# Delta-rule stage: ScalarE takes the key squares before the outputs, three engines share the copies of the inverse, and the first inverse product stands in slot 9

## The chip, the cores and the metric

One core of one Trainium2 chip. The metric is the device time of one execution in microseconds, as the median of several runs.

## What is computed

The whole program is four blocks of attention and feed-forward on x of shape 2 x 1024 x 256, each added to its input. The change lies in the attention of the last block, a gated delta rule with 32 heads of 64 and a convolution of four taps over time:

```python
mixed = lax.conv_general_dilated(mixed, conv_w, (1,), [(K_CONV - 1, 0)], ...)
...
g = -jnp.exp(A_log) * jax.nn.softplus(a + dt_bias)
beta = jax.nn.sigmoid(b)
q = _l2norm(q) * DK ** (-0.5)
k = _l2norm(k)
...
def step(Sstate, xs):
    q_t, k_t, v_t, g_t, b_t = xs
    Sstate = Sstate * jnp.exp(g_t)[..., None, None]
    kv = jnp.einsum('bhk,bhkv->bhv', k_t, Sstate)
    delta = (v_t - kv) * b_t[..., None]
    Sstate = Sstate + k_t[..., :, None] * delta[..., None, :]
    o_t = jnp.einsum('bhk,bhkv->bhv', q_t, Sstate)
    return (Sstate, o_t)
...
o = o * lax.rsqrt(var + EPS) * norm_weight * jax.nn.sigmoid(z)
return o.reshape(Bsz, Sl, VDIM) @ w_out.T
```

## The kernel before

heads3 works through 32 units: a pair of heads (16) times a sequence (2). The 1024 tokens of a unit are 16 chunks of 64. Within a chunk the recurrence is solved by the inverse of a 64 x 64 unit lower triangular matrix I + N (nT is N transposed); from chunk to chunk a state st of 64 x 64 for each head is carried.

The program is a software pipeline written out by hand. Each engine has its own instruction list, made of start, step and end, and meets the others only through counting semaphores; each engine works strictly in the order of its list. A call of step(t, u, f, p) serves four units at once: p is being projected and convolved, f gets its decays, its N and its inverse, u runs through its 16 states, t is normalised, gated and projected out. The loop body is two steps; on TensorE it is cut in the middle of a step, between slots 7 and 8 (CUT), so that its loop branch falls there in every second unit.

TensorE's step has two halves. The key side (key_side) transposes the keys of f, sums its decays (decay), and interleaves the products of keys of f (key_products) with the products of the inverse of u with values and keys (values_and_keys, key_sums). Then states runs 16 slots c = 0 to 15. In each slot the state of chunk c comes in (across), the products of the next chunk that need no state follow (within), and then beside(c) puts other work in: projections, the inverse of f, the output of t. A state needs the one before it, so across(c) waits for VectorE's update of state c, called state c or q = c - 1 here.

The inverse of f goes so: ScalarE copies the diagonal 32 x 32 blocks of nT together in y (compacted, four copies by quarters of the partitions), VectorE transposes and folds them down to 16 x 16 blocks (diagonals, gather), GpSimd solves these by 15 double steps on [128, up to 64] elements (solve) and writes them scaled as xm and xmT (sided), VectorE transposes them back (scatter) to xx. TensorE doubles them with products of 32 x 32: inverse_y, then VectorE masks; inverse_z and inverse_zt, and VectorE subtracts (refined); inverse_below, a copy into y, inverse_above, a copy into xT. These copies were ScalarE's alone (inverse_pieces): two into y, four of xx into xT, a table load, two of the product above into xT. values_and_keys of the next step needs xT whole.

Other orders that the change touches: on ScalarE, outputs (copies and squares of the finished outputs, banks 4 and 5) ended a step, and key_squares began the next; its query_squares wait for GpSimd's squares (the sum of output squares and query terms). On GpSimd a step is squares, scaled (decay times beta), gated, solve, sided, gates. PSUM banks 2 and 3 (B3), 0 and 1 (A3), 4 and 5 (C3), 6 and 7 (D3) are shared out by hand; POUT names the banks of the four output projections.

## Time and profile before

| | |
|---|---|
| median of 3 runs | 5064.07 us (5057.12 to 5071.15) |
| the profiled execution | 5072.44 us, its span 5070.4 us |
| TensorE matmul (PE) busy | 4314.5 us, 85% |
| VectorE (DVE) busy | 2256.2 us, 44% |
| ScalarE (ACT) busy | 1796.4 us, 35% |
| GpSimd (POOL) busy | 1150.8 us, 23% |
| mean granted clock of TensorE | 0.870 of full |

"[1.38 <-ACT h_y L2843]" behind an instruction says that its engine stood idle for 1.38 us before it, and which instruction released it; "issue" names no one. A little product of the inverse has many matmuls, so a row with x64 is a whole group. The units of the stage take 59.7 us each; line L3060 (VectorE's copy of the first state) occurs once in each.

### The profile page before, as it was taken

To read this page: it belongs to the slowest core of one execution; us is meant where nothing else is said; L and a number is where in the kernel's file an instruction comes from. 1 tells how busy PE (TensorE), PEld (TensorE's weight loads), DVE (VectorE), ACT (ScalarE), POOL (GpSimd) and SP (SyncE) were. 2 spreads that over 40 slices of the span, in tenths; PEclk is the share of its full clock that TensorE was granted. 3 is DMA by queue.
4 is the path that set the end of the run, shared out by engine and by line. 5 is a ranking of instruction groups with operands and counts; after the bars stand their busy time and mean duration, and the time that the engine had idled before them with its cause. 6 is when DMAs were issued, how large, how long until landed. Compare 5 with 4: busy or idle time off the path is not lost. (4 is left out here: it accounts for less than half of the span.)

```text
span 5070.4 us, 110954 instructions
## 1 busy us (share of the span) xinstructions
PE 4314.5 (85%) x45765; PEld 2627.0 (52%) x45824; DVE 2256.2 (44%) x3826; ACT 1796.4 (35%) x2794; POOL 1150.8 (23%) x1633
## 2 busy tenths in 40 slices
PE   7789869999967858779998789899988888889879
PEld 3233744544544634446466555555555555555547
DVE  5933244334443252431322255565556555555431
ACT  2057121221220113231110245555555555555431
POOL 2000110000015241310000144444444444444300
PEclk8689679999978967889998679998999998898878
DMA  1000000000021510000100000000000000000000
GB/s 43 1 1 1 26 33 1 9 9 0 3 86 52 173 52 0 0 21 0 51 0 5 9 7 9 8 8 8 8 8 8 8 8 8 8 8 8 6 13 17
DMA packets 37871, 91.96 MB, mean 18 GB/s; under 512 B 6914, under 2 KB 27173, under 8 KB 33920
## 3 DMA queue, kind: packets, MB, share of 16 engines
q1 hardware_dynamic: 27072, 69.45, 4.0%
q0 software_dynamic: 6144, 11.62, 0.8%
q8 instruction: 386, 6.32, 0.5%
q10 hardware_dynamic: 4224, 4.19, 0.3%
q14 instruction: 45, 0.37, 0.0%
HBM read 69.96 MB, written 20.45 MB: 18 GB/s over the span
## 5 line engine op out<-in xcount | busy, mean ns | idle before, releaser
L2426 PE MATMUL ps<-h_normT,h_w 128*128 128x512 f32 (+1 forms) x1008 | 456.1, 560 | 62.2 <-DVE h_xx L3001 55.9
L2943 DVE SCALAR_TENSOR_TENSOR h_cv<-h_raw,h_cw,h_cv 128x1023 f32<-128x1023 f32 (+2 forms) x288 | 371.3, 1299 | 22.3 <-ACT h_cv L2776 19.6
L3062 DVE SCALAR_TENSOR_TENSOR h_st<-h_st,d_gcs,ps 128x64 f32<-128x64 f32 x448 | 125.0, 279 | 493.8 <-PE ps L2701 493.3
L2775 ACT ACTIVATE h_raw<-ps 128x512 f32<-128x512 f32 x192 | 114.8, 598 | 529.9 <-PE ps L2426 529.0
L2335 POOL TENSOR_TENSOR h_gm<-h_gm,h_tmp 128x15 f32<-128x15 f32 (+7 forms) x480 | 260.5, 543 | 37.6
L2343 POOL TENSOR_TENSOR h_sq<-h_sq,h_qsq 128x512 f32<-128x512 f32 x64 | 79.9, 1270 | 806.8 <-ACT h_sq L2922 806.8
L877 PE MATMUL ps<-a_probT,a_v 128*128 128x512 f32 x512 | 232.5, 613 | 25.1 <-DVE a_probT L939 25.1
L2426 PEld LDWEIGHTS ps<-h_normT,h_w 128*128 128x128 f32 x1008 | 172.7, 201 | 156.1 <-issue 137.0
L854 PE MATMUL ps<-a_qkT 128*128 128x512 f32 x512 | 230.0, 593 | 3.1 <-DVE a_v L930 3.1
L2701 PEld LDWEIGHTS ps<-h_st,h_mT 64*64 64x64 f32 x1792 | 93.5, 137 | 245.3 <-issue 239.7
L1922 PE MATMUL ps<-h_normT,e_wgu 128*128 128x512 f32 (+1 forms) x448 | 204.3, 600 | 5.2 <-DMA e_wd<-in_e_wd 4.0
L2334 POOL TENSOR_TENSOR h_tmp<-h_gm 128x15 f32<-128x15 f32 (+7 forms) x480 | 179.0, 373 | 129.2 <-DVE h_gm L2988 94.1
L944 DVE TENSOR_REDUCE a_nmax<-ps 128x1 f32<-128x1024 f32 x64 | 78.4, 1224 | 240.3 <-PE ps L854 240.3
L2701 PE MATMUL ps<-h_st,h_mT 64*64 64x64 f32 x1792 | 152.6, 247 | 36.7 <-issue 27.4
L877 PEld LDWEIGHTS ps<-a_probT,a_v 128*128 128x128 f32 x512 | 99.1, 196 | 149.7 <-issue 120.1
L1086 POOL MEMSET r_zero<- 128x2048 f32 x1 | 1.8, 1804 | 766.3 <-POOLq L54 766.3
L2496 PE MATMUL ps<-h_wo,h_o 128*128 128x256 f32 x512 | 170.7, 452 | 5.5 <-DVE h_o L3007 3.8
L407 ACT ACTIVATE a_prob<-ps 128x1024 f32<-128x1024 f32 (+1 forms) x192 | 153.9, 810 | 59.9 <-PE ps L335 21.2
L448 DVE TENSOR_REDUCE a_mx<-ps 128x2 f32<-128x1024 f32 (+2 forms) x192 | 169.0, 950 | 1.8 <-PE ps L296 1.0
L909 ACT ACTIVATE a_prob<-ps,a_nbias 128x1024 f32<-128x1024 f32 x64 | 71.3, 1114 | 275.4 <-DVE a_nbias L946 275.4
L2705 PE MATMUL ps<-h_pT,h_st 64*64 64x64 f32 x1920 | 166.1, 252 | 0.5 <-DVE h_st L3062 0.5
L148 PE MATMUL ps<-ident,h_norm 128*128 128x128 f32 x256 | 48.7, 378 | 134.2 <-DVE h_norm L127 134.2
(515 smaller groups left out, 9587.2 us busy)
## 6 DMA issues: line engine op xcount, KB each, us to landing
m_wgu<-in_m_wgu SPq DMA_DIRECT2D x8, 1408.0 KB
h_w<-in_d_w SPq DMA_DIRECT2D x48, 128.0 KB, 2.1
m_wd<-in_m_wd SPq DMA_DIRECT2D x8, 704.0 KB
m_rows_in<-r_zero SPq DMA_DIRECT2D x4, 1024.0 KB, 12.2
e_xe<-m_rows_in SPq DMA_DIRECT2D x8, 512.0 KB
m_rows_out<-e_y ACTq DMA_DIRECT2D x8, 512.0 KB, 11.4
e_wgu<-in_e_wgu SPq DMA_DIRECT2D x1, 3520.0 KB
a_t_raw<-in_t_w SPq DMA_DIRECT2D x4, 768.0 KB, 4.4
```

The costliest lines, as they stand in the source:

```text
L407: act.activation(prob[:, u % 3, :, c0:BANK], ps[:, 2 * (u % 3):2 * (u % 3) + 2, c0:BANK], ACT.Exp, scale=1.0 / float(np.sqrt(D0))).then_in ...
L448: dve.tensor_reduce(mx[:, b * NQ + qt, part, m:m + 5:4], ps[:, 2 * (n % 3):2 * (n % 3) + 2, 0:w], AX.X, ALU.max).then_inc(mx_ready, 1)
L854: last = pe.matmul(ps[:, 2 * (n % 2) + half, :], qkT[:, 0, k, n * P:(n + 1) * P], qkT[:, 1, k, b * S + half * BANK:b * S + (half + 1) * BANK],
L877: last = pe.matmul(ps[:, 6 + m, :], v[:, b * NQ + kt, m * P:(m + 1) * P], probT[:, blk % 2, kt, :], start=(kt == 0), stop=(kt == NQ - 1))
L1922: last = pe.matmul(ps[0:m, 3 * (n % 2) + s, :], wgu[:, k, s, c * P:c * P + m], hT[:, k, tok], start=(k == 0), stop=(k == KC - 1))
L2334: c.link(pool.tensor_tensor(part, column, row, ALU.mult))
L2335: c.link(pool.tensor_tensor(target, target, part, ALU.subtract))
L2426: last = pe.matmul(ps[:, PROJ[m], lo:hi], w[:, kind, k, :], hT[:, k, b * S + tb * BANK + lo:b * S + tb * BANK + hi], start=(k == 0), stop= ...
L2496: last = pe.matmul(ps[:, POUT[k], j * H:(j + 1) * H], o[:, tile * P:(tile + 1) * P], wo[:], start=True, stop=True)
L2701: last = pe.matmul(ps[rows(h), D3 + c % 2, 0:HALF], mT[rows(h), c, :], st[rows(h), c, :], start=False, stop=True, tile_position=(64 * h, 6 ...
L2705: last = pe.matmul(res(h, c), st[rows(h), c, :], pT[rows(h), c, :], start=False, stop=True, tile_position=(64 * h, 64 * (1 - h)))
L2943: dve.scalar_tensor_tensor(out=d, in0=raw[:, kind, 0:S - back], scalar=tap(pr, kind, TAPS3 - 1 - back), in1=d, op0=ALU.mult, op1=ALU.add). ...
```

## The change

- TensorE: inverse_y stands in slot 9 instead of 10 and the value transposes in slot 8 instead of 9. The output projections 1, 2, 3 of t go from slots 8, 11 and 13 to 10, 12 and 13, with other banks (POUT). inverse_z goes to slot 11, inverse_zt to 12, inverse_below to 13, ahead of output projection 3; inverse_above stays in 14, alone.
- ScalarE: key_squares and decays come first in a step, then outputs of t, then the first wc and u copies and one query square; the second query square stands behind decays_upto. compacted makes three of four quarters; inverse_pieces loads its table first and makes one of two copies into y, two of four from xx, one of two from the product above.
- GpSimd: solve begins with the fourth quarter of compacted (waiting for gated and for nT), spread makes the other two copies of xx into xT behind gates.
- VectorE: the last quarter of the copy into y (below, in slot 14) and of the product above (above, at the end of the step); nT's second half is made ahead of the paired product of the second half; the transposes (scatter) move from slot 10 to 8, values to 9, masked to 10, the second gate to 11, the additions and convolutions by a slot or two.

The diff, cut to its core (the waits of the first and last steps, of start and of end are left out):

```diff
         MEAN = (A3, A3 + 1)
-        POUT = (B3 + 1, B3 + 1, A3, A3)
+        POUT = (B3 + 1, A3, A3, B3)
         UW = (D3, C3)
         KK = (A3, B3)
...
+        one = lambda r: ct[quarter(r), SUM.start + r // 2 * HALF:SUM.start + r // 2 * HALF + 1].unsqueeze(1).broadcast_to([32, NC3, DB2])
         SUBS = 2 * DB3 - 1
         blocks = lambda v: v.rearrange("p c (h j) -> p j h c", h=2)
...
                     pool.wait_ge(dec_d, 2 * n + 2)
                     pool.tensor_tensor(dec[:, grp(g), :], dec[:, grp(g), :], per_chunk(bep[:, grp(g)]), ALU.mult).then_inc(db_d, 1)
-            def solve(f):
+            def solve(f, t=None):
                 n = f[0]
                 c = Chain(pool, sub, SUBS * n)
                 eye = ct[:, EYE3]
+                pool.wait_ge(rz, 2 * t[0] + 2) if t else pool.wait_ge(db_d, 2 * n + 2)
+                pool.wait_ge(nt_d, 2 * n + 2)
+                pool.tensor_tensor(y[quarter(3), :, :], nT[quarter(3), :, side(3)], one(3), ALU.mult).then_inc(nc3_d, 1)
+                pool.wait_ge(nc3_d, n + 1)
                 pool.wait_ge(eg_p, 2 * n + 2)
                 c.link(pool.tensor_tensor(xb, eye, eye, ALU.mult))
...
                     c.link(pool.tensor_tensor(target, target, part, ALU.subtract))
                 assert c.n == SUBS
+            def spread(f, p):
+
+                pool.wait_ge(gm_d, 2 * p[0] + 2) if p else pool.wait_ge(xm_d, 2 * f[0] + 2)
+                pool.wait_ge(x_d, 2 * f[0] + 2)
+                for r in (1, 3):
+                    pool.tensor_tensor(xT[quarter(r), :, side(r)], xx[quarter(r), 1, :, :], one(r), ALU.mult).then_inc(xt_d, 1)
+                pool.wait_ge(xt_d, 2 * f[0] + 1 + r // 2)
+
             def squares(t):
                 n, pr, b = t
...
                     last.then_inc(wk, 1)
+                if t:
+                    hold(xa, 4 * n)
                 if f:
                     hold(ev, 6 * f[0] + 6)
                     hold(x_d, 2 * n + 2)
                     turn_keys(f)
-                if t:
-                    hold(xa, 4 * n)
-                if f:
                     hold(y4_d, 2 * n + 2)
                     decay(f)
-                hold(xtx, 6 * n + 6)
+                hold(xtx, 4 * n + 4)
+                hold(xt_d, 2 * n + 2)
                 hold(v_ev, n + 1)
                 if t:
...
-                    if c == 8 and t:
-                        pe.wait_ge(xa, 4 * n + 1)
-                        project_out(t, 1)
-                    if c == 9 and f:
+                    if c == 8 and f:
                         hold(ev, 6 * p[0] + 4) if p else hold(lnd, 2 * t[0] + 2)
                         turn_values(f)
-                    if c == 10 and f:
+                    if c == 9 and f:
                         if p:
-                            pe.wait_ge(xa, 4 * n + 2) if t else pe.wait_ge(ev, 6 * p[0] + 2)
+                            pe.wait_ge(xa, 4 * n + 1) if t else pe.wait_ge(ev, 6 * p[0] + 2)
                         hold(zv, 2 * n + 2)
                         inverse_y(f, (lambda k: project(p, 4, k)) if p else None)
-                    if c == 11 and t:
+                    if c == 10 and t:
                         pe.wait_ge(v_ev, f[0] + 1) if f else pe.wait_ge(lnd, 2 * t[0] + 2)
-                        project_out(t, 2)
-                    if c == 12 and f:
+                        project_out(t, 1)
+                    if c == 11 and f:
                         hold(v_ev, f[0] + 1)
                         inverse_z(f, (lambda k: project(p, 5, k)) if p else None)
+                    if c == 12:
+                        if t:
+                            pe.wait_ge(xa, 4 * n + 2)
+                        if f:
+                            hold(ev, 6 * p[0] + 5) if p else hold(xa, 4 * n + 1)
+                            inverse_zt(f, (lambda k: out_part(t, 2, k // 2) if k % 2 else None) if t else None)
+                        elif t:
+                            project_out(t, 2)
                     if c == 13:
+                        if f:
+                            inverse_below(f)
                         if t:
-                            pe.wait_ge(xa, 4 * n + 3)
-                        if f:
-                            hold(ev, 6 * p[0] + 5) if p else hold(xa, 4 * n + 2)
-                            inverse_zt(f, (lambda k: out_part(t, 3, k // 2) if k % 2 else None) if t else None)
-                        elif t:
+                            pe.wait_ge(ev, 6 * p[0] + 6) if p else pe.wait_ge(zv, 2 * n + 2)
                             project_out(t, 3)
                     if c == 14 and f:
-                        inverse_below(f)
                         inverse_above(f)
...
             def inverse_pieces(f):
                 n = f[0]
+                act.preload_act_table(ACT.Exp)
                 act.wait_ge(nx, 2 * n + 2)
-                for r in (1, 3):
-                    act.activation(y[quarter(r), :, :], small(BELOWB)[quarter(r)], ACT.Copy).then_inc(y4_d, 1)
+                act.activation(y[quarter(1), :, :], small(BELOWB)[quarter(1)], ACT.Copy).then_inc(y4_d, 1)
                 act.wait_ge(x_d, 2 * n + 2)
-                for r in range(4):
+                for r in (0, 2):
                     act.activation(xT[quarter(r), :, side(r)], xx[quarter(r), 1, :, :], ACT.Copy).then_inc(xtx, 1)
-                act.preload_act_table(ACT.Exp)
                 act.wait_ge(tt, n + 1)
-                for r in (0, 2):
-                    act.activation(xT[quarter(r), :, DB2:HALF], small(ABOVEB)[quarter(r)], ACT.Copy, scale=-1.0).then_inc(xtx, 1)
+                act.activation(xT[quarter(0), :, DB2:HALF], small(ABOVEB)[quarter(0)], ACT.Copy, scale=-1.0).then_inc(xtx, 1)
             def start(f, p):
...
                 if f:
                     key_squares(f)
                     decays(f)
-                for g in range(2):
-                    parts(g)
-                    if f:
-                        query_squares(f, g, t)
+                if t:
+                    outputs(t)
+                parts(0)
+                if f:
+                    query_squares(f, 0, t)
+                parts(1)
                 if f:
                     act.wait_ge(sse_d, f[0] + 1)
                 for g in range(2):
                 if f:
                     compacted(f)
                     decays_upto(f)
+                    query_squares(f, 1, t)
                 if p:
                     projected(p, 0)
...
                     projected(p, 5)
                 if f:
                     inverse_pieces(f)
...
-
-            def outputs(t, u):
-                n = u[0]
+
+            def outputs(t):
+
+                n = t[0]
                 chunks = lambda v, a: v.rearrange("p (j a n) -> p a j n", a=2, n=CH3)[:, a]
                 for a in range(2):
-                    act.wait_ge(o_p, NC3 * n + NC3 - 1 + a)
-                    if t and a == 0:
-                        act.wait_ge(y_p, 4 * t[0] + 4)
+                    act.wait_ge(o_p, NC3 * n + NC3)
...
                 dve.wait_ge(kk, 2 * n + g + 1)
                 dve.wait_ge(db_d, 2 * n + g + 1)
                 dve.tensor_tensor(parted(nT[:, grp(g), :]), src[:, :, :, 0, :], parted(dec[:, grp(g), :]), ALU.mult).then_inc(nt_d, 1)
+
+            def decayed_pairs(f, g):
+
+                n, pr, b = f
+                src = wide(KK[g])
                 dve.tensor_tensor(parted(ka[b][:, grp(g), 1, :]), src[:, :, :, 1, :], parted(dec[:, grp(g), :]), ALU.mult).then_inc(at_d, 1)
             def diagonals(f):
                 n = f[0]
-                dve.wait_ge(nc_d, 4 * (n + 1))
...
                 dve.wait_ge(xy, 2 * f[0] + k + 1)
                 dve.tensor_tensor(xx[:, k], xx[:, k], small((ZB, ZTB)[k]), ALU.subtract).then_inc(x_d, 1)
+
+            def below(f):
+
+                dve.wait_ge(nx, 2 * f[0] + 2)
+                dve.tensor_scalar(y[quarter(3), :, :], small(BELOWB)[quarter(3)], 1.0, None, ALU.mult).then_inc(y4_d, 1)
+
+            def above(f):
+
+                dve.wait_ge(tt, f[0] + 1)
+                dve.tensor_scalar(xT[quarter(2), :, DB2:HALF], small(ABOVEB)[quarter(2)], -1.0, None, ALU.mult).then_inc(xtx, 1)
             def start(f, p):
...
                     convolve(f, 6)
                     keys(f)
                     decayed(f, 0)
+                    decayed_pairs(f, 0)
+                    decayed(f, 1)
                 for g in range(2):
                     dve.wait_ge(mt_d, 2 * n + g + 1)
                     dve.wait_ge(qe_d, 2 * n + g + 1)
                     dve.tensor_tensor(parted(pT[:, grp(g), :]), wide(UW[g])[:, :, :, 1, :], parted(qe[b][:, grp(g), :]), ALU.add).then_inc(pt_d, 1)
                     if f and g == 0:
-                        decayed(f, 1)
+                        decayed_pairs(f, 1)
                 for q in range(NC3 - 1):
                     dve.wait_ge(s_p, (NC3 - 1) * n + q + 1)
...
                         convolve(f, q + 5)
                     if t and q == 5:
                         gate(t, 0)
-                    if t and q in (7, 9):
-                        add(t, (q - 7) // 2)
-                    if t and q == 9:
-                        gate(t, 1)
-                    if f and q == 10:
+                    if t and q == 7:
+                        add(t, 0)
+                    if f and q == 8:
                         for k in range(2):
                             scatter(f, k)
+                    if f and q == 9:
                         values(f)
-                    if f and q == 11:
+                    if f and q == 10:
                         masked(f)
-                    if t and q == 12:
+                    if t and q == 11:
+                        add(t, 1)
+                        gate(t, 1)
+                    if f and q in (12, 13):
+                        refined(f, q - 12)
+                    if t and q == 13:
                         add(t, 2)
-                    if f and q in (13, 14):
-                        refined(f, q - 13)
+                    if f and q == 14:
+                        below(f)
                     if t and q == 14:
                         add(t, 3)
-                    if p and q in (4, 6, 8, 11, 12, 14):
-                        convolve(p, (4, 6, 8, 11, 12, 14).index(q))
+                    if p and q in (4, 6, 7, 10, 12, 14):
+                        convolve(p, (4, 6, 7, 10, 12, 14).index(q))
+                if f:
+                    above(f)
             def end(t):
                 for g in range(2):
```

## Rows read from the trace of the kernel before

**Rows 1.** Steady part: stretch, its us, busy of PE, PEld, DVE, ACT, POOL, granted clock.

```profile
2947.00:4799.00 1852.00, 1648.24 (x33324) 1058.38 (x33350) 1063.73 (x1619) 1029.07 (x1621) 812.28 (x1266) 0.90 0.03 8
```

**Rows 2.** TensorE's waits there: line waited for, total us, times, longest.

```profile
PE ps L2426 <- DVE h_xx L3001: 55.9, 30, 3.4
PE ps L2414 <- ACT h_y L2843: 42.9, 31, 1.4
PE ps L2701 <- issue: 27.4, 13, 2.9
PE ps L2679 <- DVE h_pT L3054: 13.2, 31, 1.5
```

**Rows 3.** Timeline of TensorE, slots 8 to 10: odd unit first, then even.

```profile
3867.65 0.69 PE L2426 MATMUL ps<-h_normT,h_w 128*128 128x256 f32 x2 [1.76 <-DVE h_xx L3001]
...
3923.18 1.13 PE L2496 MATMUL ps<-h_wo,h_o 128*128 128x256 f32 x4
3924.66 1.16 PE L2444 MATMUL ps<-d_const,h_cv 64*64 64x64 f32 x64
3928.17 0.67 PE L2426 MATMUL ps<-h_normT,h_w 128*128 128x256 f32 x2 [1.99 <-DVE h_xx L3001]
```

**Rows 4.** Timeline of GpSimd and VectorE, same stretch, odd unit first.

```profile
3861.43 1.29 POOL L2359 TENSOR_TENSOR h_wc<-h_gm,d_const 128x512 f32<-128x512 f32 x1 [0.16 <-POOL h_gm L2335]
...
3923.58 1.28 POOL L2335 TENSOR_TENSOR h_gm<-h_gm,h_tmp 128x15 f32<-128x15 f32 x1
3925.02 1.30 POOL L2359 TENSOR_TENSOR h_wc<-h_gm,d_const 128x512 f32<-128x512 f32 x1 [0.16 <-POOL h_gm L2335]
...
3923.50 1.28 DVE L2943 SCALAR_TENSOR_TENSOR h_cv<-h_raw,h_cw,h_cv 128x1021 f32<-128x1021 f32 x1
3926.99 1.92 DVE L3001 STREAM_TRANSPOSE h_xx<-h_wc 128x512 f32<-128x512 f32 x2
```

**Rows 5.** Timeline of the key side of the odd unit, engine by engine.

```profile
3827.53 2.12 PE L2444 MATMUL ps<-d_const,h_cv 64*64 64x64 f32 x64
3834.46 1.10 PE L2479 MATMUL ps<-h_cv 64*64 64x128 f32 x32 [0.68 <-ACT h_dec L2802]
3835.36 1.83 PE L2405 MATMUL ps<-h_norm,h_xT 64*64 64x128 f32 x30
3838.55 1.10 PE L2479 MATMUL ps<-h_cv 64*64 64x128 f32 x32 [0.37 <-DVE h_norm L2959]
...
3830.36 0.60 ACT L2921 ACTIVATE h_o<-ps 128x512 f32<-128x512 f32 x1
3831.81 0.62 ACT L2922 ACTIVATE h_sq<-ps 128x512 f32<-128x512 f32 x1
3835.32 1.06 ACT L2815 ACTIVATE h_qsq<-h_cv 64x1024 f32<-64x1024 f32 x1
3841.34 2.58 ACT L2822 ACTIVATE h_y<-h_nT 32x512 f32<-32x512 f32 x4 [0.17 <-DVE h_nT L2973]
...
3832.57 2.50 POOL L2343 TENSOR_TENSOR h_sq<-h_sq,h_qsq 128x512 f32<-128x512 f32 x2 [21.89 <-ACT h_sq L2922]
3835.88 2.04 POOL L2318 TENSOR_TENSOR h_dec<-h_dec,h_bep 128x512 f32<-128x512 f32 x2 [0.81 <-DVE h_bep L2955]
...
3844.05 1.06 DVE L2981 STREAM_TRANSPOSE h_gm<-h_y 128x512 f32<-128x512 f32 x1 [0.81 <-ACT h_y L2822]
```

**Rows 6.** Timeline at the end of a unit, slot 14.

```profile
3887.15 1.20 PE L2414 MATMUL ps<-h_xx,h_y 32*32 32x32 f32 x64 [1.38 <-ACT h_y L2843]
...
3885.80 1.20 ACT L2843 ACTIVATE h_y<-ps 32x512 f32<-32x512 f32 x2 [4.44 <-PE ps L2414]
...
3884.31 0.68 DVE L3024 TENSOR_TENSOR h_xx<-h_xx,ps 128x512 f32<-128x512 f32 x1
```

**Rows 7.** Busy time and granted clock of two even units.

```profile
3786.20:3843.00 56.80, 51.63 (x1089) 33.24 (x1082) 34.80 (x53) 33.58 (x54) 26.56 (x41) 0.94 0.01 3
4143.00:4202.80 59.80, 54.74 (x1086) 34.70 (x1083) 34.78 (x54) 33.67 (x54) 26.77 (x42) 0.89 0.01 2
```

More of the change, by code:

```diff
@@ L2372, in start @@
                 gates(p)
+                spread(f, p)
             def step(t, u, f, p):
@@ L2381, in step @@
                 if f:
-                    solve(f)
+                    solve(f, t)
                     sided(f)
@@ L2385, in step @@
                     gates(p)
+                if f:
+                    spread(f, p)
             def end(t):
@@ L2820, in compacted @@
                 act.wait_ge(nt_d, 2 * n + 2)
-                for r in range(4):
+                for r in range(3):
                     act.activation(y[quarter(r), :, :], nT[quarter(r), :, side(r)], ACT.Copy).then_inc(nc_d, 1)
@@ L2924, in end @@
             def end(t):
+                outputs(t)
                 logs(t)
@@ L2978, in diagonals @@
                 n = f[0]
-                dve.wait_ge(nc_d, 4 * (n + 1))
+                dve.wait_ge(nc_d, 3 * (n + 1))
+                dve.wait_ge(nc3_d, n + 1)
                 dve.wait_ge(eg_p, 2 * (n + 1))
```

16 lines of the change are left out of this document (8 added, 8 removed).

## Prediction

> **What bounds the kernel now.** I read the page first for the share of TensorE, then the stage alone, then who TensorE waits for, then one pair of units instruction by instruction. TensorE is busy 85% of the span, no other engine over 44% (table of the page). The stage that the change touches runs from about 2880 to 4865 us; its steady part, 31 units of 59.7 us (2947 to 4799), has TensorE busy 1648.24 of 1852.00 us, every other engine at most 1063.73 [rows 1]. So a unit is 53.2 us of TensorE work and 6.6 us in which it stands still, and only these 6.6 us, and the clock, can be won. The waits of that stretch [rows 2] show where they lie: 55.9 us for the first transposed inverse (h_xx), 42.9 us for ScalarE's copies after the product below the diagonal (h_y), 27.4 us of a gap in slot 8 that comes in every second unit (13 times, no engine named; I call these units odd and the others even) and, at the end of the key side (the stretch ahead of the first state), 13.2 us for pT. In the even units the h_xx wait is 1.99 us, in the odd ones, where the gap has already held TensorE back, less (1.76 in the one shown) [rows 3]: 13 odd ones sum to about 21 us, the other 55.9 - 21 = 35 us are 1.97 in each of 16 units and 3.4 in the first.
>
> **The change, part by part.**
>
> *Inverse product one slot forward.* Product y moves from slot 10 to slot 9, the value transposes from 9 to 8, the output projections one slot or more back. TensorE therefore comes to the product earlier by one projection with its slot: 3924.66 - 3923.18 = 1.48 us in the even unit [rows 3]. What it waits for must come earlier by as much. That is GpSimd's forward solve, its scaled copy xm, and VectorE's transpose. Today xm is there at 3925.02 + 1.30 = 3926.32, and VectorE starts the transposes at 3926.99, because its own order puts a state and a gate first: 0.67 us are lost in VectorE's queue [rows 4]. With the transposes after state 8 that loss is gone. The solve itself starts earlier, relative to the first state: VectorE's block transpose waits 0.81 us for ScalarE's four copies of nT (2.58 us); now there are three, with GpSimd's beside them, 0.65 us less on ScalarE, and nT's second half is made ahead of the paired product, so about 0.8 us are won [rows 5]. Together 0.67 + 0.8 = 1.47 against 1.48: in an even unit the wait of 1.97 us stays. One thing eats a further gain: the convolution now ordered in slot 7 meets the end of the solve in every unit. In the even unit a step of 15 elements took 1.28 us under VectorE's convolution (3923.50, 1.28 us) [rows 4]; in the odd unit xm was started at 3861.43, before the convolution of slot 8, and will meet the one of slot 7, about 1 us. I count this as included in even units (they already pay it) and as the reason why the odd ones don't get far ahead. In an odd unit, xm today ends at 3862.72 and would be 0.8 earlier but 1.0 later by the convolution; plus 1.03 for the transpose and 0.15 to TensorE: 3864.1. TensorE would be there at 3867.65 - 1.76 - 1.48 = 3864.4 [rows 3]. No wait is left: -21 us over 13 units.
>
> *Copies shared, end of the unit.* ScalarE's two copies took 1.20 us and TensorE waited 1.38 [rows 6]. Now ScalarE copies one quarter (0.60) and VectorE the other. VectorE takes it behind state 14: in the unit shown the instruction behind that state starts at 3884.31 and takes 0.68 [rows 6], so the copy in its place ends at 3884.99 and TensorE goes on at 3885.15; it would be ready at about 3884.1, when its small products began there. What is late next is thus VectorE's copy, not ScalarE's: a wait of 1.04 for one of 1.38, -0.34 in each of 31 units, -10.5 us. The last output projection, between the products below and above, hides ScalarE's copy whole; without it 0.60 would be on the path. GpSimd's two copies of xT have from the second refinement to the value products, over 6 us of TensorE work; by the nearest row (two operations of one input tile and a broadcast, 2.04 us) they take 2.0 to 2.6 [rows 5], and cost nothing.
>
> *Key squares first, outputs later.* ScalarE's key squares leave the queue behind four xT copies, a table load and the four output copies, so VectorE's key chain starts some 2.6 us earlier.
>
> What is last now is GpSimd, because the outputs move behind the decays. Take K, the start of the key transposes, at 3827.53; the value products of group 0 end at K + 6.3 and those of the decays at K + 4.5, by the timeline. The decays' exponentials can start then and take 1.13; four output copies, 1.93 (from 3830.36 to the last start 3831.81 and its 0.62 today), end at K + 7.6 instead of K + 4.9. Value products of group 1 write the banks that they free: TensorE would be there at K + 7.0, so +0.75 with the hand-over. GpSimd's squares (2.50) then end at K + 10.2, ScalarE's query squares (1.06) wait for them and stand ahead of the second pair of wc/u copies (1.1): these end at K + 12.3. TensorE does value products (1.83), key sums and key products (1.10 each) meanwhile [rows 5] and would want them at K + 11.4: +1.0 with the hand-over. Against these 1.75 go the waits of today in that unit, 0.68 for the decays and 0.37 for the keys [rows 5]: +0.7. Where a key side runs at the lower clock, TensorE comes later and the first of the two waits is hidden, as are those of today: about +0.45. I take +0.55 us a unit, +17 us over 31. Behind the waiting query squares stand the second wc/u copies, the mT copies and the compaction, which is why the stall is passed on. GpSimd's scaling (2.04) moves from K + 8.35 to K + 10.2, yet nT's second half still comes 0.6 earlier, since it no longer stands behind other products.
>
> Bounds of this part, which no row shows directly: if the output copies slip in before TensorE needs the bank (no +0.75) it is -0.2 a unit; if both waits come on top with nothing gained, +1.75. I take +0.55, near the unit laid out. GpSimd's new copy of nT's last quarter (1.0 to 1.3 us by its 128x512 forms [rows 4, 5]) ends at about K + 15.9 beside ScalarE's K + 16.0; a VectorE operation in its way would make it up to 1.3 later. The Trainium skill, SBUF — State Buffer, "SBUF: two separate sides", says that GpSimd is blocked for the whole of a VectorE instruction with two SBUF inputs; the 1.28 us of a 15-element step agrees. At the new copy VectorE reads PSUM, so by the rule it isn't blocked, and by the row of the convolution it would be.
>
> *Clock.* An even unit at a granted clock of 0.94 is 56.80 us, one at 0.89 is 59.80 [rows 7]: a second stretch at 1.2 GHz costs 3.0 us. Most odd units have one too, after the gap or after the h_xx wait. With one of the two pauses gone some of them go; nothing shows how many, from none to all: 0 to 13 x 3.0 = 39 us. I take a quarter, -10 us, since the gap of slot 8 remains.
>
> The sum: -21 - 10.5 + 17 - 10 = -25 us. The profiled execution was 5072.4 us (span 5070.4), 8 over the median of 5064.07; the same difference on the median gives 5039.
>
> **The rivals.**
> (1) The solve gets well ahead: GpSimd meets fewer convolutions because it starts earlier, the even waits go too (-32 us), and with them most second stretches at the lower clock (-30 more). For it: a step of the solve is 0.3 us when free and 1.28 when blocked, so a small shift can save 1 us. Against: the transposes can't start before state 8, and the VectorE operations on SBUF are the same in number. 5039 - 32 - 30 = 4977.
> (2) No effect: the odd units' gain is eaten by key-side waits at +1.0 instead of +0.55 a unit (+14 us) and the clock gives nothing (+10): 5063. This is also the case in which the change doesn't do what it says: the key squares are early but nT is not, since the scaling on GpSimd now stands behind later squares.
> (3) Slower: the chain outputs, GpSimd squares, query squares, second wc/u copies is the bound of the key side. It decides once both waits add in full (+1.75 a unit), that is 1.2 x 31 = 37 us over my sum, and the clock gives nothing (+10): 5039 + 47 = 5086. The clock can add to it: the key side follows a stretch at 1.2 GHz in nearly every unit, and pauses there can lengthen it. The Trainium skill, TensorE: Matmul & The Clock Gate, "What's actually happening", has the low level as the default that activity lifts, by which this rival and the first would both be larger.
>
> **How the numbers follow.** Forecast 0.40 (5025 to 5055), rival 1 0.22, rival 2 0.20, rival 3 0.18. The 0.3% that a measurement of this kernel can tell is 15 us: under 5049 is faster, over 5079 slower. Of the forecast 0.32 lies under 5049 and 0.08 over; of rival 2, 0.03 and 0.17; rivals 1 and 3 count whole. Faster 0.57, same 0.25, slower 0.18. The range leaves out the far half of rival 1 and the far end of rival 3: 4978 to 5086.
>
> **What would show it.** In the trace after: PE's wait for h_xx near 2 us in even units and gone in odd ones (sum about 32 us for 55.9); instead of the wait for ScalarE's h_y one of about 1.0 for a VectorE copy; new PE waits in the key side ahead of the second value products (for ScalarE's h_sq, some 0.7) and ahead of the second key sums (for h_u, about 1.0); ScalarE idle before the query squares, with GpSimd as the releaser; xm of GpSimd done 19.9 us after the first state in even units, for 3926.32 - 3905.55 = 20.8 today. Wrong would be: no wait for h_u in the key side (then the time is lower), h_xx waits gone in all units (rival 1), or h_xx waits unchanged in odd units (rival 2 or 3).

## The result, and the profile after

The changed kernel is slower: 5102.75 us (median of 7 runs) for 5067.51 us of before, a ratio of 1.0073 with a 95% interval of 1.005 to 1.0095. A second comparison, in another group of runs, gave 1.0085 (1.0053 to 1.0117). The forecast was 5039 us and a range that ended at 5086. The profiled execution is one of the quicker ones, 5092.8 us, with a span of 5091.0.

The page of the changed kernel, its busy times (before: TensorE 4314.5, VectorE 2256.2, ScalarE 1796.4, GpSimd 1150.8):

```profile
PE 4327.9 (85%) x45824; PEld 2621.7 (51%) x45824; DVE 2294.2 (45%) x3890; ACT 1688.0 (33%) x2634; POOL 1239.9 (24%) x1729
```

ScalarE lost 108 us, which went to GpSimd (89) and VectorE (38). TensorE has the same matmuls and is still the only engine near its limit. From the first state of the first unit to that of the last the stage took 1887.2 us, for 1852.1 before. So the stage is 35.1 us longer in the profiled executions, while the rest of the program, where nothing was changed, was 14.5 us shorter in them. The kernel before has this one trace; a second one of the changed kernel has a stage of 1896.5 us.

Whom TensorE waits for in the steady part, changed kernel (line waited for, total us, times, longest), to be held against [rows 2]. This view begins 27 us behind the first state of the stage; over the whole stage the row of h_xx is 34.8 us, 17 times, since the first unit has a wait of 3.9 us:

```profile
PE ps L2430 <- DVE h_y L3051: 36.4, 31, 1.2
PE ps L2593 <- ACT h_u L2887: 35.0, 31, 1.2
PE ps L2442 <- DVE h_xx L3023: 30.9, 16, 2.4
PE ps L2460 <- issue: 30.6, 54, 1.4
PE ps L2719 <- issue: 28.8, 13, 2.8
PE ps L2512 <- issue: 17.0, 23, 1.4
PE ps L2421 <- ACT h_sq L2937: 10.9, 19, 0.7
```

Every wait that was forecast is here, near its size: h_xx in the 16 even units alone (30.9 for a forecast of 32; over the whole stage 34.8 from 55.9), VectorE's copy instead of ScalarE's (1.2 us each), the wait for ScalarE's u copy ahead of the second key sums (1.2) and the one for h_sq (0.7). What was not forecast is "issue" on the transposes (L2460) and the output projections (L2512), and the clock. This is an odd unit of the changed kernel, TensorE from slot 7 on:

```profile
3744.42 1.02 PE L2451 MATMUL ps<-h_normT,h_wz 128*128 128x512 f32 x2
3747.97 1.11 PE L2460 MATMUL ps<-d_const,h_cv 64*64 64x64 f32 x59
3750.14 0.48 PE L2460 MATMUL ps<-d_const,h_cv 64*64 64x64 f32 x5 [1.06 <-issue]
3751.26 1.22 PE L2442 MATMUL ps<-h_normT,h_w 128*128 128x256 f32 x2
3752.41 0.65 PE L2430 MATMUL ps<-h_xx,h_nT 32*32 32x32 f32 x32
...
3758.82 2.07 PE L2512 MATMUL ps<-h_wo,h_o 128*128 128x256 f32 x4
```

The h_xx wait ahead of 3751.26 is gone, as forecast. But the projection takes 1.22 us where 0.70 is the time at full clock, and so it stays through the output projection, 2.07 us for 1.13 in [rows 3]. Busy time and granted clock (last column but two) of this stretch, then of an even and of an odd unit of the same kernel:

```profile
3749.00:3763.00 14.00, 12.94 (x216) 8.02 (x211) 6.53 (x10) 1.17 (x2) 2.46 (x3) 0.51 0.01 2
4046.50:4102.90 56.40, 50.94 (x1091) 32.20 (x1083) 36.05 (x56) 30.30 (x49) 29.16 (x45) 0.97 0.01 3
3728.20:3793.10 64.90, 58.05 (x1087) 36.54 (x1083) 36.33 (x56) 30.26 (x49) 29.44 (x45) 0.84 0.04 13
```

A clock of 0.51 over 14 us is the 1.2 GHz level nearly all through. I summed the time at that level, called the low clock from here on, from the granted clock in the traces, for units 1 to 29, and split it 36 us after the first state: the first part holds the slots up to about 11, the second the end of the unit and the next key side. All in us a unit; "pauses" is the sum of TensorE's idle gaps of over 0.15 us.

| kernel | length | low clock, first 36 us | low clock, rest | pauses |
|---|---|---|---|---|
| before | 60.05 | 4.71 | 6.71 | 6.14 |
| changed | 61.32 | 7.77 | 4.35 | 6.55 |
| changed, again | 61.63 | 7.57 | 5.02 | 6.76 |

In odd units the first part went from 5.0 to 11.0 us. Over the whole stage, from the first state of the first unit to that of the last, TensorE stood idle for 213.7 us (203.8 before) and was busy for 1673.5 (1648.4 before) with the same matmuls.

### The profile page after: what moved, and what is told of

Its sections match the earlier page's. It is cut to its first block and busy times, and to the rows that moved or that the text cites. A ratio compares the mean times of both kernels' runs of the same rounds, so it can differ in the third digit from the quotient of the medians.

```text
span 5091.0 us, 111110 instructions
## 1 busy us (share of the span) xinstructions
PE 4327.9 (85%) x45824; PEld 2621.7 (51%) x45824; DVE 2294.2 (45%) x3890; ACT 1688.0 (33%) x2634; POOL 1239.9 (24%) x1729
## 5 line engine op out<-in xcount | busy, mean ns | idle before, releaser
L2442 PE MATMUL ps<-h_normT,h_w 128*128 128x512 f32 (+1 forms) x1008 | 478.4, 584 | 41.7 <-DVE h_xx L3023 34.8
L2340 POOL TENSOR_TENSOR h_gm<-h_gm,h_tmp 128x15 f32<-128x15 f32 (+7 forms) x480 | 239.2, 498 | 37.6
L2339 POOL TENSOR_TENSOR h_tmp<-h_gm 128x15 f32<-128x15 f32 (+7 forms) x480 | 213.3, 444 | 90.1 <-DVE h_gm L3010 55.0
L2348 POOL TENSOR_TENSOR h_xT<-h_xx,d_const 32x512 f32<-32x512 f32 x64 | 66.2, 1034 | 527.4 <-DVE h_xx L3046 525.0
L2512 PE MATMUL ps<-h_wo,h_o 128*128 128x256 f32 x512 | 169.4, 449 | 22.9 <-issue 17.0
L2719 PE MATMUL ps<-h_st,h_mT 64*64 64x64 f32 x1792 | 156.2, 252 | 36.9 <-issue 28.8
L944 DVE TENSOR_REDUCE a_nmax<-ps 128x1 f32<-128x1024 f32 x64 | 78.4, 1225 | 240.4 <-PE ps L854 240.4
```

The source lines that it names most:

```text
L2339: c.link(pool.tensor_tensor(part, column, row, ALU.mult))
L2340: c.link(pool.tensor_tensor(target, target, part, ALU.subtract))
L2442: last = pe.matmul(ps[:, PROJ[m], lo:hi], w[:, kind, k, :], hT[:, k, b * S + tb * BANK + lo:b * S + tb * BANK + hi], start=(k == 0), stop= ...
L2512: last = pe.matmul(ps[:, POUT[k], j * H:(j + 1) * H], o[:, tile * P:(tile + 1) * P], wo[:], start=True, stop=True)
L2719: last = pe.matmul(ps[rows(h), D3 + c % 2, 0:HALF], mT[rows(h), c, :], st[rows(h), c, :], start=False, stop=True, tile_position=(64 * h, 6 ...
```

## The experiments

The ratios below are to the kernel before in the same group of runs on one chip. Its median was 5073.34, 5112.12, 5075.33 and 5104.72 us in the four groups, so times of different groups are not set against each other. The ratios are estimated from all the runs of a group and can differ from the quotient of the two medians by up to 0.0014. The low clock and the waits of a kernel are those of its one profiled execution.

### Group 1: slots, ScalarE's order, one projection, the query squares

**The slots alone.** The kernel before, with TensorE's slots, banks and VectorE's order of the changed one:

```diff
 # before, plus
-        POUT = (B3 + 1, B3 + 1, A3, A3)
+        POUT = (B3 + 1, A3, A3, B3)
-                    if c == 10 and f:
+                    if c == 9 and f:
...
                         inverse_y(f, (lambda k: project(p, 4, k)) if p else None)
```

> The kernel before with only the slots moved (TensorE's order, its banks, VectorE's order), copies and ScalarE's order as before. Theory S, the slots: with output projection 1 out of slot 8, the loop gap, the value transposes and the first inverse product stand side by side, TensorE gets the lower clock there for longer in odd units (11 us a unit for 5), and this alone makes the kernel slower: about 5100 for 5067 before, low clock in the first 36 us of odd units over 9 us. Theory K, the key side: the loss is made by ScalarE's new order (waits of 1.2 and 0.65 us), so without it this kernel is faster than before by the h_xx waits of odd units (21 us) and by ScalarE's copies that the last output projection now hides (up to 1.2 x 31 = 37): 5010 to 5045.

5063.25 us, 0.9982 (0.9964 to 1.0). Both theories miss. The low clock of the first part is there, 8.69 us a unit, more than in the changed kernel. But at the end of the unit it fell to 1.31, and the wait for h_y is gone from the list. TensorE's waits of this kernel:

```profile
PE ps L2426 <- DVE h_xx L3000: 46.2, 17, 4.5
PE ps L2479 <- ACT h_dec L2801: 35.9, 23, 1.8
PE ps L2444 <- issue: 32.7, 62, 1.3
PE ps L2702 <- issue: 30.8, 13, 3.1
PE ps L2496 <- issue: 9.8, 21, 0.8
```

So the slots take away at one end of the unit what they give at the other.

**The rest alone.** The changed kernel with the slots put back (copies shared, ScalarE's new order):

```diff
 # changed, plus
-        POUT = (B3 + 1, A3, A3, B3)
+        POUT = (B3 + 1, B3 + 1, A3, A3)
-                    if c == 9 and f:
+                    if c == 10 and f:
...
                         inverse_y(f, (lambda k: project(p, 4, k)) if p else None)
```

> The changed kernel with the slots of TensorE and VectorE put back, keeping the shared copies and ScalarE's new order. Theory S: the loss goes, 5050 to 5075, low clock in the first 36 us of odd units back near 5 us. Theory K: the loss stays, about 5100, since the waits ahead of the key sums (1.2 us, 31 times) and of the second value products stay.

5082.04 us, 1.0018 (0.9999 to 1.0036): most of the way back, though 7 us above the range of theory S. The low clock in the first part of odd units is 6.5 us. Neither half makes the loss alone; 0.9982 and 1.0018 multiply to 1.0000, and together they are 1.0073 and 1.0085.

**Output projection 1 back in slot 8.**

```diff
 # changed, plus
-        POUT = (B3 + 1, A3, A3, B3)
+        POUT = (B3 + 1, B3 + 1, A3, B3)
+                    if c == 8 and t:
+                        pe.wait_ge(xa, 4 * n + 1)
+                        project_out(t, 1)
                     if c == 8 and f:
...
-                    if c == 10 and t:
-                        pe.wait_ge(v_ev, f[0] + 1) if f else pe.wait_ge(lnd, 2 * t[0] + 2)
-                        project_out(t, 1)
```

> The changed kernel with output projection 1 alone put back in slot 8, ahead of the value transposes; the inverse products stay one slot forward. Theory S: the dense projection behind the gap keeps the clock, odd units lose most of their low stretch, h_xx waits fall from 1.9 to about 0.5 us in even units since TensorE comes 1.1 later: 5040 to 5065. Theory K: no change against the changed kernel, 5090 to 5105.

5040.81 us, 0.9934 (0.9909 to 0.996), as theory S has it, and faster than both kernels. The low clock of the first part is 0.64 us a unit instead of 7.77 (in the rest of the unit it rose from 4.35 to 6.18); the pauses are the same, 6.64 for 6.55. Units 1 to 29 at a granted clock of 0.94 for 0.90:

```profile
2998.90:4720.10 1721.20, 1523.06 (x31382) 967.32 (x31378) 1045.46 (x1595) 877.89 (x1393) 848.23 (x1277) 0.94 0.03 8
```

**The query squares out of the way.**

```diff
 # changed, plus
                 parts(0)
-                if f:
-                    query_squares(f, 0, t)
                 parts(1)
...
                     decays_upto(f)
+                    query_squares(f, 0, t)
                     query_squares(f, 1, t)
```

> The changed kernel with both query squares of ScalarE behind the decays up to, so that nothing between the outputs and the second wc and u copies waits for GpSimd. Theory K: the wait ahead of the second key sums (35.0 us in all) goes and with it most of the loss, 5060 to 5075. Theory S: the wait goes, but the time falls by no more than it, since the low stretch in slots 8 to 10 stays: 5070 to 5095.

5106.72 us, 1.0056 (1.0036 to 1.0076): outside both ranges, and no clear gain on the 1.0073 of its base. The wait of the key sums is gone; in its place stand waits for pT (14.9 us, 30 times) and for the paired product (7.7), and the low clock rose to 14.0 us a unit. From the start of the key transposes to the first state it is 16.28 us on average, for 16.40 with the wait.

### Group 2: useless work, and VectorE's copy

**The same four matmuls once more.** Their result goes to a bank that the next projection overwrites; the output is unchanged.

```diff
 # changed, plus
+                    if c == 8 and t:
+                        pe.wait_ge(xa, 4 * n + 1)
+                        for j in range(2):
+                            pe.matmul(ps[:, B3 + 1, j * H:(j + 1) * H], o[:, (2 + j) * P:(3 + j) * P], wo[:], start=True, stop=True)
                     if c == 8 and f:
```

> The changed kernel plus useless work: in slot 8, ahead of the value transposes, the four matmuls of output projection 1 run once more into a bank that nobody reads (the first inverse's projection overwrites it); all else, the result too, is the same. That is 1.13 us more for TensorE in each of 31 units, 35 us if nothing else changes. Theory S, now as the granted clock (a sparse stretch from the loop gap through the value transposes brings the low level): the extra dense work keeps the clock and the time falls in spite of it, to 5060 to 5085 for about 5105; low clock in the first 36 us of a unit under 3 us for 7.8. Rival (the loss is a matter of the banks, of VectorE's order or of instruction supply): 5130 to 5140.

5071.71 us, 0.9918 (0.9894 to 0.9943), in theory S's range, where the changed kernel is 1.0073 and 1.0085: more work, about 1.5% less time. The steady part (units 1 to 29) of the changed kernel and of this one, each as stretch, us, busy times, granted clock:

```profile
2995.30:4773.40 1778.10, 1583.84 (x31383) 997.77 (x31378) 1047.79 (x1595) 877.45 (x1393) 848.16 (x1276) 0.90 0.03 8
```

```profile
3049.30:4750.00 1700.70, 1527.71 (x31473) 973.19 (x31494) 1046.74 (x1596) 877.98 (x1393) 848.77 (x1277) 0.95 0.03 8
```

TensorE has 116 more weight loads, and is busy for 56 us less, at a granted clock of 0.95 for 0.90. The low clock of the first part is 0.47 us a unit for 7.77. The banks, VectorE's order and the slots of the inverse are those of the changed kernel, so none of these by itself brings the low clock. One thing moved with the extra work: TensorE comes later to the inverse, and the h_xx wait of even units is 0.9 us for 1.9.

**Both copies below the diagonal on ScalarE.**

```diff
 # changed, plus
-                act.activation(y[quarter(1), :, :], small(BELOWB)[quarter(1)], ACT.Copy).then_inc(y4_d, 1)
+                for r in (1, 3):
+                    act.activation(y[quarter(r), :, :], small(BELOWB)[quarter(r)], ACT.Copy).then_inc(y4_d, 1)
...
-                    if f and q == 14:
-                        below(f)
```

> The changed kernel with both copies of the product below the diagonal on ScalarE again, as before; VectorE's below is gone. Theory: VectorE's copy stands behind state 14 and is what TensorE waits for (1.2 us, 36.4 in all), and it keeps the low clock at the end of the unit; ScalarE's two copies are hidden by the last output projection. Time falls by 25 to 50 us to 5055 to 5080, low clock after 36 us of a unit from 4.4 towards the 1.3 us of the kernel with the slots alone. Rival (the wait is only passed on, as when the query squares were moved): 5095 to 5105.

5061.22 us, 0.9898 (0.9874 to 0.9921). The wait fell from 36.4 us to 2.4:

```profile
PE ps L2593 <- ACT h_u L2888: 36.7, 31, 1.2
PE ps L2442 <- DVE h_xx L3024: 34.3, 17, 3.8
PE ps L2460 <- issue: 32.2, 61, 1.1
PE ps L2719 <- issue: 25.0, 13, 2.6
PE ps L2421 <- ACT h_sq L2938: 19.1, 30, 0.7
PE ps L2512 <- issue: 17.1, 23, 1.7
...
PE ps L2430 <- ACT h_y L2860: 2.4, 2, 1.4
```

and the low clock after 36 us from 4.35 to 1.18 us a unit, in the first part from 7.77 to 4.59. The trace flatters this kernel: it is the fastest of six executions, 5040.27 us at a mean clock of 0.884, and the median of the six clocks is 0.878. Why the first part has less of the low clock too, with projection 1 still in slot 10, no run shows.

**Both together.** Edits of the two above.

> Output projection 1 in slot 8 and both copies on ScalarE, on top of the changed kernel. If the two effects add, 25 to 50 us less than the kernel with the projection alone (5041): 4990 to 5020. If the unit only stops elsewhere, 5035 to 5045.

5016.1 us, 0.9804 (0.9781 to 0.9827), the lowest ratio: low clock 0.66 and 3.81 us a unit. The two edits took 1.4% and 1.7% off the changed kernel one by one, and 2.7% together.

**The same slots on ScalarE's old order.** The slots-alone kernel with projection 1 in slot 8.

> The kernel before with the slots moved, output projection 1 kept in slot 8, and ScalarE's order and copies as before. Theory K', that ScalarE's new order costs 0.4 us a unit or more in the key side whatever the slots: faster than the kernel with both, 4980 to 5010. If the new order pays once the clock is kept, it is slower than that one: 5020 to 5040.

5056.2 us, 0.9877 (0.9846 to 0.9909), slower than the 0.9804 in the same group, as the second theory has it, though outside both ranges. So ScalarE's new order with its shared copies is not the loss. The 0.7% is not its gain alone, though, for the clock was not kept here: the median of the six executions' mean clocks is 0.882, for 0.890 of the kernel with both. In the trace, which is the slowest of the six, the low clock is 5.81 and 4.54 us a unit, and it lies in the even units, 8.19 us of their first part, with the projection in slot 8. One of them, and the same place in the kernel with ScalarE's new order and projection 1 in slot 8 (TensorE's busy time is the second figure behind a stretch, the granted clock the last but two):

```profile
3588.94 1.13 PE L2496 MATMUL ps<-h_wo,h_o 128*128 128x256 f32 x4
3590.00 1.16 PE L2444 MATMUL ps<-d_const,h_cv 64*64 64x64 f32 x64
3593.17 0.67 PE L2426 MATMUL ps<-h_normT,h_w 128*128 128x256 f32 x2 [1.57 <-DVE h_xx L3000]
...
3594.60:3625.30 30.70, 29.81 (x597) 20.16 (x598) 10.91 (x17) 11.68 (x19) 1.92 (x3) 0.50 0.01 3
```

```profile
3551.59 1.13 PE L2512 MATMUL ps<-h_wo,h_o 128*128 128x256 f32 x4
3552.65 1.16 PE L2460 MATMUL ps<-d_const,h_cv 64*64 64x64 f32 x64
3555.16 0.67 PE L2442 MATMUL ps<-h_normT,h_w 128*128 128x256 f32 x2 [0.91 <-DVE h_xx L3023]
...
3553.00:3570.00 17.00, 13.95 (x478) 9.48 (x470) 8.71 (x13) 3.63 (x5) 3.96 (x4) 1.00 0.02 4
```

The work is the same and in the same order; the wait ahead of the inverse is 1.57 us in the one and 0.91 in the other. The first goes to the low clock a microsecond and a half later, for 30.7 us, of which TensorE is busy 29.81; the second stays at full clock.

### Group 3: the loop branch, and the key side again

**The changed kernel itself.**

> The changed kernel itself once more, to stand on the same chip as the three others of this group: 1.005 to 1.010 of before.

5120.86 us, 1.0085 (1.0053 to 1.0117).

**The loop cut in another place.**

```diff
-            CUT = 8
+            CUT = 5
```

> The changed kernel with TensorE's loop cut between slots 4 and 5 instead of 7 and 8, so that the pause of the loop branch falls among the dense projections; the order of the work is the same. If the pause next to the value transposes is what brings the low clock, odd units lose their 11 us of it and the time falls by 20 to 40 us, a ratio to before of 0.999 to 1.003. If the sparse products alone bring it, it stays within 0.3% of the changed kernel.

5104.93 us, 1.0055 (1.0035 to 1.0075): above the first theory's range, and 0.3% under the changed kernel, the edge of the second's. The low clock of odd units in the first part fell from 11.0 to 5.3 us, so the place of the pause has a share in it, but over all units it is 12.4 a unit, as before the edit (12.1): the even units and the ends of the units got it instead. And the branch now has two pauses, before and behind slot 5:

```profile
PE ps L2705 <- issue: 30.2, 13, 2.4
PE ps L2719 <- issue: 25.6, 13, 2.3
```

**The fastest kernel with the same cut.**

> The kernel with output projection 1 in slot 8 and both copies on ScalarE (0.980 of before), with the loop cut between slots 4 and 5. The low clock in the first 36 us is nearly gone there already (0.66 us a unit), so the place of the pause should be worth no more than 0.3%: 0.977 to 0.983. The h_xx waits may come back in odd units, since the pause no longer gives the solve time behind slot 7, but it still comes ahead of it.

5011.99 us, 0.9866 (0.9844 to 0.9889), worse than expected. Even units are at full clock from end to end and take 54.34 us on average; odd ones carry the two pauses and 8.1 us of the low clock, and take 62.57.

**The fastest kernel with one query square moved.**

> The same kernel (0.980 of before) with the first query square directly behind the second wc and u copies instead of ahead of them. The wait ahead of the second key sums (36.7 us in all) goes. If the key side is on the path, 20 to 35 us less, 0.973 to 0.977. If the wait moves on to pT and the paired products, as it did when both squares were put last, 0.979 to 0.983.

4989.27 us, 0.9823 (0.9799 to 0.9847), in the range of the wait that moves on. It is the lowest time of all, in a group where the kernel before has 5075.33.

### Group 4: what was still open

**Its base on the same chip, and once more itself.**

> Output projection 1 in slot 8 and both copies on ScalarE once more, as the base of the next one: 0.980 to 0.987 of before.

> The same with the first query square behind the second wc and u copies, on the same chip. The profile shows 36 us less of waits for ScalarE's u copy and 27 us of new ones (pT and the paired product). If only the difference counts, 5 to 15 us less than the run beside it (0.2%); if the wait was a real cost, 25 us or more less.

5006.56 us, 0.9806 (0.9782 to 0.9831), and 5012.38 us, 0.9811 (0.9787 to 0.9835): the same, so neither of the two gains expected for the moved square came. The wait of 36.8 us for u gives way to pT (16.8) and the paired product (10.8), yet the key side is 0.47 us a unit shorter, 14.72 for 15.19. What it won is gone by the end of the unit: the pauses differ by 0.1 us, and the low clock of the first part is 1.69 us a unit for 0.72.

**VectorE's copy in the kernel before.**

```diff
 # before, plus
-                for r in (1, 3):
-                    act.activation(y[quarter(r), :, :], small(BELOWB)[quarter(r)], ACT.Copy).then_inc(y4_d, 1)
+                act.activation(y[quarter(1), :, :], small(BELOWB)[quarter(1)], ACT.Copy).then_inc(y4_d, 1)
...
                         refined(f, q - 13)
+                    if f and q == 14:
+                        dve.wait_ge(nx, 2 * f[0] + 2)
+                        dve.tensor_scalar(y[quarter(3), :, :], small(BELOWB)[quarter(3)], 1.0, None, ALU.mult).then_inc(y4_d, 1)
```

> The kernel before with one change: of the two copies of the product below the diagonal the one of the last quarter is VectorE's, behind state 14 and the second refinement, ScalarE keeps the other. By the prediction's step the wait of 1.38 us becomes about 1.0, -10 us, 0.996 to 1.000 of before. If VectorE's copy costs by its place in VectorE's queue whatever the slots, 1.003 to 1.010.

5103.18 us, 0.9993 (0.9978 to 1.0008). The wait is 26.4 us for 42.9 before, and the ratio lies in the first theory's range, but no gain can be told from none. In the traces the pauses are 5.41 us a unit for 6.14, and the low clock 12.8 for 11.4, which takes most of it back.

## Why the prediction was wrong

**Inverse product one slot forward: right.** Forecast: 1.97 us of wait left in each even unit, none in the odd ones. Measured: 30.9 us, 16 times, none in odd units; with the first unit's wait 34.8 for 55.9, -21 as forecast. In the even unit from 4046.5 xm was done at 4065.17 + 1.29, 19.96 us after the first state; the forecast said 19.9. GpSimd:

```profile
4065.17 1.29 POOL L2372 TENSOR_TENSOR h_wc<-h_gm,d_const 128x512 f32<-128x512 f32 x1 [0.16 <-POOL h_gm L2340]
```

**Copies shared: mechanism right, size a little off.** The wait is 1.2 us and not 1.04, so 42.9 became 36.4: -6.5 for -10.5. What the step left out is the alternative. It compared VectorE's copy with ScalarE's two copies in the old slots. In the new slots the last output projection stands in between and hides both of ScalarE's copies (2.4 us of wait in all). So the copy on VectorE lost about 34 us of waits that the slot move would have won, and some of the clock behind them: with it the changed kernel stands at 1.0073, without it at 0.9898, while in the old slots the same copy moved nothing (0.9993). This is why the two halves of the change, harmless alone, lose together. I had written that this projection hides ScalarE's copy whole, and did not ask what it would hide if nothing were moved to VectorE.

**Key side: right.** Forecast +0.55 us a unit from the two new waits. Measured: the second key sums wait 1.2 us (31 times), the second value products 0.7 (19 times), and from the start of the key transposes to the first state 16.40 us for 15.95, +0.45. ScalarE stood idle ahead of the query square, with GpSimd as releaser, and VectorE for 3.9 us for the scaled decays, as laid out (ScalarE, GpSimd, VectorE of the changed kernel):

```profile
3787.42 1.06 ACT L2831 ACTIVATE h_qsq<-h_cv 64x1024 f32<-64x1024 f32 x1 [1.78 <-POOL h_sq L2356]
...
3784.80 2.50 POOL L2356 TENSOR_TENSOR h_sq<-h_sq,h_qsq 128x512 f32<-128x512 f32 x2 [11.79 <-ACT h_sq L2937]
3787.25 2.05 POOL L2319 TENSOR_TENSOR h_dec<-h_dec,h_bep 128x512 f32<-128x512 f32 x2
...
3788.41 0.69 DVE L2989 TENSOR_TENSOR h_nT<-ps,h_dec 128x512 f32<-128x512 f32 x1 [3.92 <-POOL h_dec L2319]
```

GpSimd's copy of nT took 1.04 us, the lower end. It ran beside VectorE's addition for pT, which reads PSUM, and was not held up. The rule in the Trainium skill, SBUF — State Buffer, "SBUF: two separate sides", has it so. Rival 3, that this chain turns the sign, is refuted: it needed 1.75 us a unit here, and the key side grew by 0.45. Two kernels without the key sums' wait are no faster than their bases either.

**The sum of the named waits was nearly right.** Over the whole stage of the two traces, h_xx is -20.4 (both its rows), h_y -6.5 and the key side +16.2, together -11; the forecast had -14.5. (The key side's terms: before 13.2 for pT, 10.4 for the decays, 7.2 for the keys and 0.4 for u, 31.2 in all; after 35.0 for u, 10.9 for h_sq and 1.5 for pT, 47.4.) By these alone the change would have been a small gain.

**Clock: the step that failed.** I priced a low stretch rightly (3.0 us for 6.8 us at the low level, 0.44 each) and took its number to follow the pauses: one pause fewer in odd units, so -10 us. The number followed the work in between as well. Output projection 1 had stood, dense, between the loop pause and the value transposes. With it moved two slots on, z projection, loop pause, 64 transposes of 64 columns, a state and then products of 32 x 32 between small projections follow each other, and the low level holds for up to 13.6 us.

What the first 36 us of a unit have, in us a unit, from one trace each:

| kernel | odd: pauses | odd: low clock | even: h_xx wait | even: low clock |
|---|---|---|---|---|
| changed | 3.20 | 11.0 | 1.9 | 5.1 |
| projection 1 back in slot 8 | 3.50 | 1.3 | 0.9 | 0.1 |
| projection repeated | 2.64 | 1.1 | 0.9 | 0.0 |
| projection 1 in slot 8, ScalarE's old order | 3.41 | 2.9 | 1.6 | 8.2 |

In odd units the pauses are no shorter with the projection in slot 8, and the low clock all but goes: there the work between decides. In even units the later start also halves the h_xx wait, and in the last row, with the projection in slot 8 but a wait of 1.6 us, the low clock stays. So there the length of the pause counts, and the projection alone is not enough. The pauses of a whole unit are 6.55 us with the projection in slot 10 and 6.64 with it in slot 8, so their sum tells nothing of the clock. The Trainium skill, TensorE: Matmul & The Clock Gate, "HAM oscillation — how this bites in real kernels", ties the low level to idle gaps: the even units agree, while in the odd units 11.0 and 1.3 us of it stand against pauses of 3.20 and 3.50.

From the changed kernel to that with both copies on ScalarE the stage lost 104 us, 24 of them pauses; the other 80 for 197 us less at the low level are 0.41 each. The repeated projection gives the same: 73 us less, with 35 added and 22 of pauses gone, over 211 us: 0.41. In the balance of before and changed kernel the end of the unit got better while the first part got worse: (7.77 - 4.71) + (4.35 - 6.71) = +0.7 us a unit, some 9 us at this price. This is too low, for in the kernel before more of the low level fell into waits, in which no matmul runs. In time in which TensorE was busy the low level was 340.8 us of the stage before and 373.6 after, +33. Between the changed kernel and that with both copies on ScalarE TensorE's busy time fell by 79.5 us for 176.3 us less of this, 0.45 each. By that price, an estimate, the clock cost some 15 us where I had -10.

**A term that was missing: "issue".** Pauses that name no one sum to 59.3 us in the steady part before (27.4, 11.5, 11.4 and 9.0) and to 78.4 after (28.8, 30.6, 17.0 and three small ones), +19 us; a new wait of the transposes for the last convolution (h_cv, 4.6 us) was not in the sum either. The prediction put such new pauses at nothing. They grew on the transposes of 64 small matmuls (11.5 to 30.6), which in the odd units now come straight behind the loop pause (1.06 inside them in the unit shown), and on the output projections (none listed before, then 17.0). With the extra projection ahead of them the transposes' share fell to 23.4. What these pauses are no run shows.

So of the 35 us in the stage, TensorE's idle time is +10 (forecast waits -11, h_cv +5, "issue" +19, small ones -3), the clock about +15, and 10 us are busy time of TensorE that I can't assign. Against the forecast's -25 the clock was 25 us off, the waits 24 and this rest 10.

**The rivals.** None of the three was it. The measured size came near rival 3, by another mechanism. Rival 1 named the clock as the large lever, but tied it to the solve getting ahead; in fact the levers are one dense projection and one copy, and they are larger than I priced: with both put back 5102.75 x (0.9804 / 1.0073) is about 4966 by ratios of two groups, below the range's low end. That is another kernel than the one forecast.

## What to carry to other kernels

Where TensorE is the bound and does much small work, a plan of slots is also a plan of the clock: before a dense product is moved out of a sparse stretch, list what then stands side by side and how long the waits next to it are, and price it from rows at both levels. When work is handed to another engine, compare with what the other edits of the same change would already hide. A wait that ends in a chain over three engines was not won in either of two tries by removing its last link: look at what arrives next.

## What the runs showed that I had not expected

Work added to the bounding engine made the kernel faster: 1.13 us more in each of 31 units, and the stage took 1814.0 us instead of 1887.2. And the place of a loop branch is not free: cut between slots 7 and 8 TensorE paused once in the odd units (28.8 us, 13 times), between 4 and 5 twice (30.2 and 25.6). TensorE also stayed at the low clock for 30.7 us in a stretch in which it was busy for 29.81.

The kernel before itself had medians from 5067.51 to 5112.12 us in different groups, 0.9%, as much as the effect; two groups on one chip had 5075.33 and 5104.72, so it is not the chip alone. Only ratios inside a group could carry the comparison.
